# A one-core graph-network kernel: another table of batches, with the heavy single places two batches later

## The reference, cut to what matters

```
h = relu(layernorm(x))                                  # 6250 x 256
out1 = segment_sum(edge_attr, dst)                      # 6250 x 96
out2 = segment_max(edge_attr, dst), 0 where no edge
out3 = out1 / max(count, 1)
c = concat([h, out1, out2, out3, u[0]])                 # 6250 x (256 + 3*96 + 64)
y = x + (relu(c @ W1 + b1) @ W2 + b2 + h)
```

## Time and profile before

| | us |
|---|---|
| median of 3 timed runs | 542.56 |
| profiled execution, its time | 541.06 |
| its span, first to last instruction | 539.3 |
| start of batch 0's layer 1 | 47.9 |
| start of batch 8's layer 1 (first of four tiles) | 261.9 |
| start of batch 14's layer 1 | 487.9 |
| start of batch 15's layer 1 | 508.2 |

### The profile page before, as it was taken

How to read it: one execution, slowest core, us unless ns; L and a number is a source line. 1 busy time by engine, 2 the same in 40 slices (tenths; PEclk the granted TensorE clock), 3 DMA queues, 4 the chain that set the end, 5 groups by cost and what they waited for, 6 DMA issues and landing times.

```text
span 539.3 us, 9275 instructions
## 1 busy us (share of the span) xinstructions
PE 492.8 (91%) x3179; PEld 449.9 (83%) x3179; DVE 436.9 (81%) x766; ACT 389.9 (72%) x1128; POOL 249.5 (46%) x260
## 2 busy tenths in 40 slices
PE   0497989989999999998999999999999999999990
PEld 0257989879999999997888888888888888889990
DVE  3878887999998989999998998988988978449420
ACT  1576888978888969798886876867786785564430
POOL 3257632645473757746556284363571550300211
PEclk9999999999999999999999999999999999999996
DMA  3877531546254554645556255254452450100100
GB/s 102 286 206 220 152 117 54 163 137 205 95 171 157 158 196 140 237 136 158 170 177 206 69 171 186 74 194 150 131 163 96 130 150 0 41 1 1 40 21 19
DMA packets 18836, 71.17 MB, mean 132 GB/s; under 512 B 4569, under 2 KB 5753, under 8 KB 18774
## 3 DMA queue, kind: packets, MB, share of 16 engines
q0 software_dynamic: 15408, 65.75, 38.7%
q1 hardware_dynamic: 3376, 4.79, 2.8%
HBM read 64.12 MB, written 6.85 MB: 132 GB/s over the span
## 4 chain that ended last, share of the span: by engine, by line
PE 74%; DVE 14%; issue 4%; DMA 3%; ACT 2%; POOL 0%; DVEq 0%; SPq 0%; POOLq 0%; ACTq 0%
PE l1ps L679 28%; PE l1ps L683 15%; PE yps L697 14%; PE yps L701 7%; DVE work L899 4%; PE l1ps L686 4%; DVE work L888 3%; PE tps L664 3%; DVE work L910 1%; DMA dstp<-tail 1%; DVE hl L988 1%; DVE inl L992 1%; PE tpr L667 1%; PE l1ps L639 1%; DMA work<-in_L_gnn_W 1%
## 5 line engine op out<-in xcount | busy, mean ns | idle before, releaser
L360 POOL DMA_INDIRECT work<-in_edge_attr,idx x98 | 125.1, 1277 | 166.8 <-DVE work L910 78.2
L497 ACT ACTIVATE hff<-l1ps,b1e 128x512 f32<-128x512 f32 (+2 forms) x128 | 74.8, 584 | 99.5 <-PE l1ps L686 98.1
L679 PE MATMUL l1ps<-inh,w1h 128*128 128x512 f32 (+2 forms) x512 | 116.3, 349 | 4.0 <-ACT hh L499 1.5
L683 PE MATMUL l1ps<-inl,w1h 128*128 128x512 f32 (+2 forms) x512 | 112.6, 341 | 1.8 <-DVE inl L992 1.8
L488 ACT ACTIVATE work<-work,mk 128x96 f32<-128x96 f32 x403 | 113.7, 369 | 0.0
L679 PE MATMUL l1ps<-inh,w1l 128*128 128x512 f32 (+2 forms) x512 | 112.3, 341 | 0.0
L899 DVE TENSOR_TENSOR work<-work 128x192 f32<-128x192 f32 (+9 forms) x154 | 110.4, 738 | 1.1
L379 POOL DMA_INDIRECT out_y<-xr,oidx x49 | 67.6, 1379 | 90.0 <-DVE xr L1019 73.9
L988 DVE TENSOR_TENSOR hl<-hff,hh 128x512 fp32r<-128x512 f32 (+2 forms) x128 | 72.1, 567 | 45.8 <-ACT hh L499 29.3
L697 PE MATMUL yps<-w2h,hh 128*128 128x256 f32 x392 | 99.5, 284 | 0.0
L697 PE MATMUL yps<-w2l,hh 128*128 128x256 f32 x392 | 98.2, 280 | 0.0
(11 more groups left out here) (162 smaller groups left out, 556.1 us busy)
## 6 DMA issues: line engine op xcount, KB each, us to landing
work<-in_L_gnn_W SPq DMA_DIRECT2D x2, 1024.0 KB, 6.2
work<-in_edge_attr,idx POOLq DMA_INDIRECT x98
xr<-in_L_gnn_W SPq DMA_DIRECT2D x1, 1024.0 KB
xr<-in_x,nid POOLq DMA_INDIRECT x49
out_y<-xr,oidx POOLq DMA_INDIRECT x49
work<-in_dst SPq DMA_DIRECT2D x1, 415.0 KB
dstp<-in_dst SPq DMA_DIRECT2D x1, 415.0 KB
hff<-in_L_gnn_W SPq DMA_DIRECT2D x3, 128.0 KB
```

The source lines that it names most:

```text
L360: pool.indirect_dma_start(out=runs[:, j * k * F:(j + 1) * k * F], out_offset=None, in_=edge, in_offset=bass.IndirectOffsetOnAxis(ap=idx[:, ...
L497: act.activation(hf[C % 2][:, 0:cols], l1ps[C % 2][:, 0:cols], ACT.Relu, bias=b1e[:, m:m + 1])
L679: pe.matmul(ps, wt[:, c, ks(m)], inh[b % 2][:, c, 0:cols], start=(c == 0 and wt is w1h), stop=False)
L683: pe.matmul(ps, w1h[:, c, ks(m)], inl[b % 2][:, c, 0:cols], start=False, stop=False)
```

## The change

Only the table of batches is another. There are now 17: three of two tiles as before; seven of three, the first two of which have the light tiles 10 and 11 in the single place, and the others the heavy tiles 44 to 48; four of four; and three of two, (34,35), (2,3) and (0,1). The pairs of the three-tile and four-tile batches move along.

```
--- before.py
+++ after.py
@@ -41,9 +41,9 @@
            22, 22, 23, 23, 24, 24, 24, 24, 25, 25, 27, 27, 28, 28, 29, 31, 32, 35, 40]
     assert len(LOW) == len(CAP) == PER
 
-    BATCHES = [[(4, 5)], [(6, 7)], [(8, 9)], [(10, 11), (44,)], [(12, 13), (45,)], [(14, 15), (46,)], [(16, 17), (47,)], [(18, 19), (48,)],
-               [(20, 21), (42, 43)], [(22, 23), (40, 41)], [(24, 25), (38, 39)], [(26, 27), (36, 37)], [(28, 29), (34, 35)],
-               [(30, 31), (32, 33)], [(0, 1)], [(2, 3)]]
+    BATCHES = [[(4, 5)], [(6, 7)], [(8, 9)], [(12, 13), (10,)], [(14, 15), (11,)], [(16, 17), (44,)], [(18, 19), (45,)], [(20, 21), (46,)],
+               [(22, 23), (47,)], [(24, 25), (48,)], [(26, 27), (42, 43)], [(28, 29), (40, 41)], [(30, 31), (38, 39)], [(32, 33), (36, 37)],
+               [(34, 35)], [(2, 3)], [(0, 1)]]
     NB = len(BATCHES)
     NCH = NB * HC
     groups, tiles = [], []
```

## The result

The changed kernel takes 552.07 us (median of four runs, 551.42 to 553.87) where the kernel before takes 542.54 us on the same chip: a ratio of 1.0178, with a 95% interval of 1.0155 to 1.0202. The forecast was 550.0 us in a range of 543.6 to 553.5. The change is a loss of 1.8%. The profiled execution took 551.5 us, its span 549.7 us, 10.4 us more than before.

What follows compares the result with a forecast made beforehand. TensorE, busy 91% of the span, was taken as near its limit, with VectorE setting the pace in some stages. Terms +0.1 - 1.2 + 2.0 + 6.5 = +7.4 us on the median 542.56 gave 550.0 us, range 543.6 to 553.5.

Steps and rivals of the forecast that it cites:

- TensorE itself: TensorE's own matmuls: eight more chunks but the same 49 tiles, so batch width hardly matters; +0.1 us.
- rival 4: Two-tile stages: narrow batches cost TensorE time, one more such batch adds 1.4 us, 551.4 us; chance 0.04.
- DMA: Gathers and scatters: same rows, one issue per tile, release order kept; 0 us.
- The early stages: Batch 3's lighter single place shortens VectorE's lap 2 and TensorE's wait at line 683; -1.2 us, ends 0 and -2.1.
- Rival 2: Early stages 2 and 3: the light single place frees 5 us, total -1.4 us, 541.2 us; chance 0.10.
- The heavy single places: Stages 7 to 9: VectorE's trees for heavier batches, plus light masks, cost +2.0 us, ends +1 and +3.5.
- The 0.6 us for the light masks: Stage 9: three small VectorE instructions, hidden before in a four-tile stage, now cost +0.6 us.
- The slot price: VectorE's trees: each edge slot costs 0.2 us, sum and maximum passes together.
- The end: Last two-tile stages 14 and 15: masks, statistics and tree of (0,1) hold TensorE up; +6.5 us, ends +2 and +8.
- The three waits: TensorE in stages 14 and 15: 1.5 us for in_hi, 2.4 and 2.6 us for lo behind the tree of (0,1).
- Rival 1: Last stages: a lead absorbs the end, which costs only 1 us; total +1.9, 544.5 us; chance 0.15.
- Rival 3: Stage 10: batches of four don't catch up with 98 slots ahead, 2 us more, 552.0 us; chance 0.09.

Runs made afterwards that it cites:

- e_pad64: Changed kernel with 64 already satisfied waits at the head of ScalarE's instruction list; 549.18 us, ratio 1.0142.
- i_before_pad64: Kernel before the change with the same 64 already satisfied waits at the head of ScalarE's list; 541.30 us, ratio 0.9999.
- g_spread2: Changed kernel with the masks of (0,1) moved to stage 13 (chunks 3, 4, 5, 7) and its tree spread over stages 14 and 15; 542.80 us, ratio 1.0035.
- relief variants: VectorE work moved out of or within stage 9 of g_spread2 (once also with four-tile batches reversed), or stage 7 of the kernel before; 545.48, 543.16, 544.92 us.
- d_light: Changed kernel with the three small light-mask instructions moved from stage 9 to stage 10; 552.80 us, ratio 1.0164.
- n_mended: g_spread2 with the light masks in stage 10 and the four batches of four in reverse order; 542.52 us, ratio 1.0022.
- h_rev4: Changed kernel with its four batches of four reversed, so stage 9 prepares 94 slots, not 98; 548.81 us, ratio 1.0142.
- a_again: The changed kernel once more, unaltered, for a second profile on a second chip; 552.37 us, ratio 1.0165.

## Why the prediction was right, and where it was wrong

The sign and the size were right: +7.4 us forecast, +7.8 on a chip without pauses (the spans of e_pad64 and i_before_pad64), +9.5 recorded. The mechanism was right for the largest term, the end, and in part wrong for the two others. That the sum came out within 0.4 us is partly luck: the early part brought 0.9 us less than forecast, the end cost 0.6 us less, and the middle reached its 2 us in another way. By its terms:

- *TensorE itself*, +0.1: borne out. Stage 15 of g_spread2 has two tiles and takes 19.0 us, 9.5 us per tile, as wider batches do. That ends rival 4. The spacings of the Trainium skill (TensorE: Matmul & The Clock Gate, "Back-to-back issue gap"), by which narrow matmuls cost more per column, are not what this kernel shows.
- *DMA*, 0: borne out for this change. The only waits on DMA came in the relief variants, from an edit of the order on POOL.
- *The early stages*, -1.2: **wrong, -0.3**. ScalarE was the follower as argued, and more so: in the first profile VectorE waits 1.02 us for in_hi of batch 3's second tile, and its lap 2 shrinks only from 23.1 to 22.2 us, not by 2.1. The wait of 1.61 us at line 683 became 0.47 us for in_hi and 1.49 for in_lo in e_pad64. Stages 2 and 3 together are 0.7 us shorter than in i_before_pad64, near the 0.9 that the prediction called sure; the 0.3 us taken on top of it didn't come. The larger error is a step left out: in stage 1 TensorE waits for ScalarE's high parts, and batch 3's pair now has 16 masks instead of 14. Stage 1 is 0.5 us longer (22.63 against 22.15 us). Rival 2 had its "for" in the same lap and falls with it.
- *The heavy single places*, +2.0: **right in sum (+2.1), wrong in its parts**. Stages 7 and 8 were to take 29.4 and 30.4 us and took 28.5 to 28.8, near TensorE's pace. Nearly all of it came in stages 9 and 10 (35.2 and 38.1 us in e_pad64, against 33.9 and 37.5 us for the old stages 7 and 8 in i_before_pad64). The step that failed is the reading of the earlier trace rows as laps that each cost TensorE their own excess. The old stages 5 and 6 had none of VectorE's to begin with, as shown above. And in e_pad64 VectorE's lead takes up the excess of stage 8 unseen (its lap is 29.8 us, the stage 28.5), and stage 9 pays at once, in its waits of 0.87 and 3.36 us. Stage 9 was forecast at 32.9 us from a stage 7 of 31.9; on e_pad64's chip that stage takes 33.9 us, so it grew by 1.3 us where 1.0 was forecast. Behind the long wait both have a granted clock of 0.95 over the stage, which the trace of before didn't have. The 0.6 us for the light masks is not there: d_light gives nothing back and n_mended at most 0.2 us for both its edits, since they stand behind the wait that counts. The slot price held for VectorE, but not as a price for TensorE (h_rev4).
- *The end*, +6.5: right, **the surest part**. The three waits came out within 0.3 us, and g_spread2 got 6.4 us back for moving what they wait for. Against the kernel before, the end costs 5.9 us: the last stage is 0.8 us shorter than the old one (30.3 against 31.1 us), which I had not forecast. The difference lies behind TensorE's last matmul (11.5 against 12.3 us to the end of the span), so in the last output and scatter; its cause was not looked into. Rival 1 fell.
- *Rival 3* has a little to it: stage 10 takes 38.1 us in e_pad64 where old stage 8 took 37.5, 0.6 us and not 2.
- *What the recorded run has beyond that*: e_pad64's ratio of 1.0142 against 1.0178. In the first profile the early part is 1.3 us longer than before instead of 0.3 shorter, since the wait for in_hi at 114.45 is 2.33 us and not 0.47, behind pauses of 1.0 and 0.6 us; and the waits of 1.15 and 1.03 us at the start of stages 10 and 11 follow ScalarE's pauses of 1.6 and 2.9 us. A ratio of this kernel depends by 0.3 to 0.4% on whether such pauses occur; that they, and not something else about the chip, make the difference is argued from these waits, not shown.

## What to carry to other kernels

A stage's busy times don't tell what a batch will cost, its order does: at the end of this kernel 6.4 us hung on 26 masks that stood in a stage of two tiles rather than of four and on one tree that wasn't spread over its chunks, and moving them gave all of it back with no work removed. Where stages differ in length, put the fixed work of the last batches in the longest stage that can take it, and count each queue behind each moved piece, POOL's among them. And where two engines wait for each other in turns, price the work ahead of the wait that counts; work behind it is free until that wait is gone. Last, an excess of 1 us read from one trace may be a pause of that execution and no bound: two stages that the prediction took for paced by VectorE lost theirs on another chip.

## What the runs showed of the hardware that I had not expected

**A wait can cost more than its length.** Behind TensorE's wait of 2.33 us at 114.45 the granted clock is 0.50 for the next 2.75 us, which is the lower of the two levels, 1.2 GHz.

```profile
114.45:117.20 2.75, 2.75 (x9) 2.75 (x10) 2.65 (x5) 1.10 (x4) 0.00 (x0) 0.50 0.01 1
...
307.20:310.50 3.30, 3.27 (x22) 3.30 (x23) 3.27 (x4) 0.84 (x2) 2.45 (x3) 1.00 0.48 119
```

The second row is the stretch behind the longer wait of stage 9, 3.31 us, in the same execution: the clock stayed at 1.00. In a_again, e_pad64 and g_spread2 the same wait (3.35 or 3.36 us) has a clock of 0.95 over stage 9, and four matmuls of 384 columns behind it take 1.48 us in e_pad64 where they take 0.87 later in that stage. So a wait of this size can cost more behind it: TensorE's busy time over stage 9 is 29.6 us at a clock of 1.00 (the first profile) and 31.0 at 0.95 (e_pad64), some 1.3 us more for the same matmuls. The same wait needn't do it twice. Nor need the lower clock make a stage longer: stage 3 takes 29.7 us behind the wait at 114.45, and 29.9 us in e_pad64, where the clock stays at 1.00 and TensorE waits 1.49 us for in_lo instead.

**ScalarE can stand still with nothing open**, as here before the copy of a tile whose transposes had ended at 352.84:

```profile
352.08 1.43 ACT L488 ACTIVATE work<-work,mk 128x96 f32<-128x96 f32 x5
356.37 0.60 ACT L527 ACTIVATE inh<-tps 128x512 fp32r<-128x512 f32 x1 [2.86 <-remote]
```

Such pauses of 0.5 to 2.9 us stand mostly at the same instructions in the profiles of three chips, and are absent on two others, with the list of instructions shifted or not. Only the profiles on a chip without them told them from the change, and from VectorE's part in the kernel before.
